# Last feed-forward of a four-layer kernel: its products moved to the first slots of the memory stage

## Chip, cores and metric

The kernel runs on one core of one Trainium2 chip. The metric is the device time of one execution, in microseconds. Each kernel was timed in several runs; the time before is 1814.58 us, the median of three runs (1812.86 to 1815.31).

## What is computed

Four residual sublayers follow each other; each is `x = x + layernorm(f(layernorm(x)))`. x has 4 batches of 512 rows and 256 columns, float32. The sublayers are a state-space mixer, a feed-forward with a Hadamard transform, an attention against a fixed memory, and a block of attention and eight experts. The change lies between the second and the third:

```
# second: feed-forward, hidden size 1024
hidden = silu(x @ W1.T) * (x @ W3.T)      # gate and up product
out = fwht(hidden) @ W2.T                 # transform of the 1024 columns
# third: memory attention, 8 heads of 128, memory of 256 rows, three steps
Q = layernorm(hidden) @ Wq.T ; K = mn @ Wk.T ; V = mn @ Wv.T
for _ in range(3):
    scores = einsum(xi, K) * beta
    w = entmax15(scores)                  # square(clip(x - tau, 0)), threshold tau by row
    xi = einsum(w, V)
out = xi @ Wo.T
```

## The kernel before

The rows lie in SBUF as `X`, 16 tiles of 128 rows (four tiles a batch, P = 128). The stages follow each other as blocks, each with an instruction queue written out for every engine: `layer0_block` (mixer and the feed-forwards of the first batches), `join_block` (memory weights folded into G1, G2, G3, and the gate products of the last batch), `memory_block`, `experts_block`. All waits are semaphores; nothing is scheduled by a planner.

`memory_block` works on 48 units. A unit is one step (of three) of one tile; four tiles go side by side in lanes, so unit m has lane m mod 4, and units 0 to 3 are first steps, 8 to 11 last steps, 12 to 15 first steps of the next four tiles. For a unit, TensorE makes the scores of 8 heads in four banks of PSUM (`score`, in pairs of heads), VectorE takes the eight largest of each row (`largest`, MAX8), GpSimd makes running sums of these, VectorE cuts at zero (`clear`), ScalarE takes a root, and VectorE takes the bound on the threshold (`bound`). From it GpSimd makes the first shift, and four passes refine it: ScalarE clips the scores with the shift (`clip`), VectorE takes mean and spread (`take_moments`), GpSimd makes a Newton step (`second_moment`, `newton`), with a root on ScalarE. The weights of the last pass are made by VectorE and GpSimd (`weights`), transposed by TensorE into banks TB and TB + 1 (4 and 5), and squared and copied to `wT` by ScalarE (`columns`). The next step of the tile takes its scores from `wT`; after the last step `output` makes the output rows into bank OUT (7), and `out_stats`, `out_norm` normalise and add them. Bank 6, ROWS, holds transposed input rows.

The order is by slots. Every engine runs a loop over n from -4 to 55, and each step of a unit has a fixed place in a slot with a fixed offset: in slot n TensorE makes the scores of unit n + 2 and the transposes of unit n - 1. VectorE in its slot n takes the largest of units n - 4 (last heads) and n - 3, the bound of unit n - 4, and so on; its slot n stands against TensorE's slot n - 6. An instruction waits for all that stand ahead of it in its engine's queue.

The last batch's feed-forward is spread over these slots. Its gates and its transposed rows are ready from `join_block`. `F_UP_AT` names the slots of the eight up products (0 to 7), `F_ROWS_AT` those of the four row products (8, 9, 14, 15):

- `f_up` (L1733): two matmuls of 512 columns into OUT, behind the scores of the slot.
- `f_hide` (L1353): VectorE multiplies the product into the gated rows.
- `f_rows` (L1747): eight matmuls of 256 columns into OUT for one tile, after all eight hides; the transform is in the weights by then.
- `f_stats_out` (L66, L68), `f_out_rstd` on GpSimd (L1555, L1557), `f_out` (L1365, L1368): normalise and add to X.
- The sync engine waits for `f_x_ready` of all four tiles and then loads the weights of the last stage.

`transpose` (L1723) puts one matmul on the identity ahead of each pair, the warm-up (L1716), except in some slots:

```
for _ in range(0 if a.m and Unit(a.m - 1).last or a.m + 1 in F_UP_AT + F_ROWS_AT else WARM[p]):
    pe.matmul(bank[:, TB + p % 2, 0:NMEM], ident[:], G1[:, 0, 0, :], start=True, stop=True)
```

A matmul in float32 appears as two records in the trace, each with its own weight load.

Of the kernel before, what the change touches and what calls it, by code (L numbers as in the profile page):

```python
# [18 lines left out]
ALU = mybir.AluOpType  # L19
# [3 lines left out]
P = 128  # L23
# [11 lines left out]
HT = HID // P  # L35
# [1089 lines left out]
DVE_HEADS = (0, 1, 2, 3, 4)  # L1125
POOL_HEADS = (5, 6, 7)
DVE_CLIPS = ((), (), (), (3,))
F_UP_AT = tuple(range(HT))
F_ROWS_AT = (8, 9, 14, 15)
FIRST_SLOT, LAST_SLOT = -4, TILES * STEPS - 1 + 8  # L1130

NPAIR = NHM // 2
# [19 lines left out]
def memory_block(nc, T, dram):  # L1152
# [7 lines left out]
    with ExitStack() as ctx:  # L1160
# [3 lines left out]
        def sem(name):  # L1164
# [3 lines left out]
        SC, TB, ROWS, OUT = 0, 4, 6, 7  # L1168
# [52 lines left out]
        f_up_done, f_hidden_ready, f_o_done, f_omv_ready, f_ors_ready, f_x_ready = (sem("f_" + n) for n in (  # L1221
            "up_done", "hidden_ready", "o_done", "omv_ready", "ors_ready", "x_ready"))
        block = ctx.enter_context(nc.Block())

        def out_rows(a):

# [30 lines left out]
        def _(dve):  # L1257
# [26 lines left out]
            def clear(a):  # L1284
                if not a.live:
                    return
                dve.wait_ge(room_ready, of_unit(a))
                dve.tensor_scalar(room[:, a.lane], room[:, a.lane], 0.0, None, ALU.max).then_inc(clear_ready, 1)

            def bound(a):  # L1290
                if not a.live:
                    return
                dve.wait_ge(back_ready, of_unit(a))
                dve.tensor_tensor(back[:, a.lane], back[:, a.lane], fold[0][:, a.lane, 0:NHM, PAD:], ALU.min)
                dve.drain()
                dve.tensor_reduce(neg8[:, a.lane], back[:, a.lane], AX.X, ALU.max, negate=True).then_inc(bound_ready, 1)
# [30 lines left out]
            def weights(a, *heads):  # L1327
                if not a.live:
                    return
                dve.wait_ge(shift_ready[PASSES - 1], of_unit(a))  # L1330
                for h in heads:
                    dve.tensor_scalar(u[a.lane][:, h, :], u[a.lane][:, h, :], shift[:, a.lane, h:h + 1], 0.0, ALU.add,  # L1332
                                      ALU.max).then_inc(dve_weights, 1)
# [12 lines left out]
                dve.drain()  # L1346
                dve.tensor_tensor(X[:, a.tile, :], X[:, a.tile, :], onorm[:], ALU.add).then_inc(x_ready, 1)

            def f_hide(s):
                if s in F_UP_AT:  # L1350
                    j = F_UP_AT.index(s)
                    dve.wait_ge(f_up_done, j + 1)
                    dve.tensor_tensor(hidden[j], bank[:, OUT, :], hidden[j], ALU.mult).then_inc(f_hidden_ready, 1)  # L1353

            def f_stats_out(s):
                if s in F_ROWS_AT:
                    t = F_ROWS_AT.index(s)
                    dve.wait_ge(f_o_done, t + 1)
                    norm_stats(dve, bank[:, OUT, 0:D], f_ostats, f_omv[:, t, :]).then_inc(f_omv_ready, 1)
# [26 lines left out]
            for n in range(FIRST_SLOT, LAST_SLOT + 1):  # L1386
                if n == LAST_SLOT - 3:
                    first_batch_stats()
                if n == LAST_SLOT - 1:
                    first_batch_rows()  # L1390
                largest(Unit(n - 4), 6, 7)
                take_moments(Unit(n - 5), 1, 0)
                invert(Unit(n - 6), 2)
                take_moments(Unit(n - 5), 1, 1, 2)
                weights(Unit(n - 7), 1, 2)
                tile_rows(Unit(n - 2))
                take_moments(Unit(n - 5), 1, 3)
                invert(Unit(n - 5), 1)
                weights(Unit(n - 7), 3)
                take_moments(Unit(n - 6), 3, 0)  # L1400
                f_hide(n - 6)
                f_stats_out(n - 6)
                tile_stats(Unit(n + 4))
                clear(Unit(n - 4))
                weights(Unit(n - 7), 4)
                if n - 7 == UNITS - 1:
                    weights(Unit(n - 7), 5, 6, 7)
                clip(Unit(n - 6), 3, 6)
                take_moments(Unit(n - 6), 3, 1)
                bound(Unit(n - 4))  # L1410
                clip(Unit(n - 6), 3, 7)
                take_moments(Unit(n - 6), 3, 2, 3)
                out_stats(Unit(n - 8))
                take_moments(Unit(n - 4), 0, 0)
                invert(Unit(n - 6), 3)
                take_moments(Unit(n - 4), 0, 1)
                take_moments(Unit(n - 5), 2, 0)
                out_norm(Unit(n - 8))
                f_out(n - 6)
                take_moments(Unit(n - 4), 0, 2)  # L1420
                largest(Unit(n - 3), 0, 1)
                take_moments(Unit(n - 4), 0, 3)
                weights(Unit(n - 6), 0)
                largest(Unit(n - 3), 2, 3)
                take_moments(Unit(n - 5), 2, 1)
                invert(Unit(n - 4), 0)
                take_moments(Unit(n - 5), 2, 2)
                largest(Unit(n - 3), 4)
                take_moments(Unit(n - 5), 2, 3)
                largest(Unit(n - 3), 5)  # L1430

        @block.gpsimd
        def _(pool):
# [77 lines left out]
            def start(a):  # L1511
                if not a.live:
                    return
                pool.wait_ge(bound_ready, of_unit(a))
                pool.tensor_tensor(shift[:, a.lane], neg8[:, a.lane], top[:, a.lane, :, 0], ALU.subtract).then_inc(start_ready, 1)  # L1515
# [62 lines left out]
            for n in range(FIRST_SLOT, LAST_SLOT + 1):  # L1578
                if n == LAST_SLOT - 3:
                    first_batch_norms()  # L1580
                add_room(Unit(n - 3))
                second_moment(Unit(n - 4), 1)
                step_back(Unit(n - 3))
                newton(Unit(n - 4), 1)
                start(Unit(n - 3))
                second_moment(Unit(n - 5), 3)
                tile_rstd(Unit(n + 3))
                out_rstd(Unit(n - 7))
                f_out_rstd(n - 5)
                newton(Unit(n - 5), 3)  # L1590
                if n - 5 != UNITS - 1:
                    weights(Unit(n - 5), 5)
                second_moment(Unit(n - 3), 0)
                if n - 5 != UNITS - 1:
                    weights(Unit(n - 5), 6)
                newton(Unit(n - 3), 0)
                if n - 5 != UNITS - 1:
                    weights(Unit(n - 5), 7)
                second_moment(Unit(n - 4), 2)
                centre(Unit(n - 2))  # L1600
                square(Unit(n - 2))
                running_sum(Unit(n - 2), 0)
                running_sum(Unit(n - 2), 1)
                newton(Unit(n - 4), 2)
                running_sum(Unit(n - 2), 2)
                mean_and_gap(Unit(n - 2))
                mean_square(Unit(n - 2))
                add_gap(Unit(n - 2))
# [73 lines left out]
        def _(pe):  # L1682
# [26 lines left out]
            def transpose(a, *pairs):  # L1709
                if not a.live:  # L1710
                    return
                for p in pairs:
                    if a.m * NPAIR + p >= 2:
                        pe.wait_ge(wT_ready, of_unit(a, NPAIR, p - 1))
                    for _ in range(0 if a.m and Unit(a.m - 1).last or a.m + 1 in F_UP_AT + F_ROWS_AT else WARM[p]):
                        pe.matmul(bank[:, TB + p % 2, 0:NMEM], ident[:], G1[:, 0, 0, :], start=True, stop=True)  # L1716
                    if any(h // 2 == p for h in dve_heads(a)):
                        pe.wait_ge(dve_weights, of_unit(a, len(DVE_HEADS), sum(h <= 2 * p + 1 for h in dve_heads(a))))
                    if any(h // 2 == p for h in pool_heads(a)):
                        pe.wait_ge(pool_weights, of_unit(a, len(POOL_HEADS), sum(h <= 2 * p + 1 for h in pool_heads(a))))  # L1720
                    for i in range(4):
                        h, piece = 2 * p + i // KN, i % KN
                        last = pe.transpose(bank[:, TB + p % 2, i * P:(i + 1) * P], u[a.lane][:, h, piece * P:(piece + 1) * P],  # L1723
                                            ident[:])
                    last.then_inc(wT_in_psum, 1)

            def f_up(s):
                if s in F_UP_AT:
                    j = F_UP_AT.index(s)
                    if j:  # L1730
                        pe.wait_ge(f_hidden_ready, j)
                    for k in range(KD):
                        last = pe.matmul(bank[:, OUT, :], w3[:, k, j * P:(j + 1) * P], f_xnT[:, k, :], start=k == 0,  # L1733
                                         stop=k == KD - 1)
                    last.then_inc(f_up_done, 1)

# [1126 lines left out]
```

## Time and profile before

| what | before |
|---|---|
| median of 3 runs | 1814.58 us |
| profiled execution | 1812.72 us |
| its span | 1810.9 us |
| mean granted clock of TensorE | 0.931 |
| TensorE busy, share of the span | 1557.9 us, 86% |
| VectorE busy | 1362.2 us, 75% |
| ScalarE busy | 1151.7 us, 64% |
| GpSimd busy | 751.9 us, 42% |

PE is TensorE's matmul queue, PEld its weight loads, DVE VectorE, ACT ScalarE, POOL GpSimd. PEclk is the granted clock as a share of full speed; it has two levels, 0.5 (1.2 GHz) and 1.0 (2.4 GHz), and values between are means over a stretch. Durations of neighbours on one engine overlap by a few hundredths, so what an instruction costs its queue is read from start to start. "idle before" is the engine's idle time ahead of an instruction, and the name behind the arrow is what ended it.

### The profile page before, as it was taken

How to read it: one execution, taken by the hardware profiler on the slowest of the kernel's cores; microseconds unless marked ns; L12 is line 12 of the kernel's file. 1: busy time of each engine (PE TensorE's matmuls, PEld its weight loads, DVE VectorE, ACT ScalarE, POOL GpSimd, SP SyncE). 2: the span in 40 equal slices, each digit the busy share in tenths (PEclk: the TensorE clock that was granted, in tenths of full speed). 3: DMA queues.
4: the chain of work that ended last, by engine and by line, in shares of the span. 5: the costliest groups of instructions: out<-in, count | busy, mean ns of one | idle time of the engine just before them, and what ended most of it. 6: DMA issues, size and time to landing. Idle time of an engine off the chain costs nothing. (4 is left out here: it accounts for less than half of the span.)

```text
span 1810.9 us, 25659 instructions
## 1 busy us (share of the span) xinstructions
PE 1557.9 (86%) x7346; PEld 1091.4 (60%) x7346; DVE 1362.2 (75%) x3568; ACT 1151.7 (64%) x2769; POOL 751.9 (42%) x2049
## 2 busy tenths in 40 slices
PE   5889999998577879877997789877779999999987
PEld 2546657466455668766786678666645556555554
DVE  6666757572489899999999999999644566767646
ACT  3243342413278888889989998999447565665630
POOL 3414224150356666677767776677310101001000
PEclk9699999998877899989998999899899999999989
DMA  5000000000000000030000000000000000000000
GB/s 231 1 1 1 1 1 1 1 1 0 1 1 1 1 1 1 1 112 1 1 1 1 1 1 1 1 1 1 1 1 1 1 1 1 1 13 1 13 1 24
DMA packets 6716, 19.21 MB, mean 11 GB/s; under 512 B 1072, under 2 KB 4144, under 8 KB 5296
## 3 DMA queue, kind: packets, MB, share of 16 engines
q1 hardware_dynamic: 6576, 17.58, 2.6%
q8 instruction: 60, 0.98, 0.2%
q14 instruction: 80, 0.66, 0.1%
HBM read 15.48 MB, written 2.10 MB: 10 GB/s over the span
## 5 line engine op out<-in xcount | busy, mean ns | idle before, releaser
L1316 DVE BATCH_NORM_STATS2 r_moments<-mem_arena 128x6 f32<-128x512 f32 x576 | 382.7, 683 | 4.2 <-ACT mem_arena L1638 4.1
L1638 ACT ACTIVATE mem_arena<-mem_arena,r_shift 128x256 f32<-128x256 f32 x792 | 351.3, 512 | 38.7 <-POOL r_shift L1533 38.7
L1706 PE MATMUL r_bank<-arena,r_wT 128*128 128x256 f32 x1024 | 243.8, 399 | 10.1 <-ACT mem_arena L1638 8.1
L1706 PEld LDWEIGHTS r_bank<-arena,r_wT 128*128 128x128 f32 x1024 | 203.1, 201 | 46.4 <-issue 17.2
L1723 PE MATMUL r_bank<-ident,mem_arena 128*128 128x128 f32 x576 | 107.1, 322 | 93.1 <-DVE mem_arena L1332 80.7
L1280 DVE MAX8 r_top<-r_bank 128x8 f32<-128x256 f32 x384 | 145.4, 417 | 26.5 <-PE r_bank L1706 24.3
L1723 PEld LDWEIGHTS r_bank<-ident,mem_arena 128*128 128x128 f32 x576 | 79.2, 165 | 131.0 <-DVE mem_arena L1332 65.7
L2293 ACT ACTIVATE arena<-arena,e_NM 128x512 f32<-128x512 f32 (+3 forms) x256 | 134.3, 558 | 29.2 <-DVE e_NM L1981 29.2
L1706 PE MATMUL r_bank<-arena,r_xnT 128*128 128x256 f32 x512 | 122.6, 401 | 18.2 <-ACT mem_arena L1638 17.0
L1981 DVE CUSTOM_DVE_ANT_0 arena<-e_banks,ffn_then_moe 128x512 f32<-128x512 f32 (+3 forms) x256 | 110.1, 485 | 28.9 <-PE e_banks L2498 28.5
L1316 DVE BATCH_NORM_STATS2 r_moments<-r_u 128x6 f32<-128x512 f32 x192 | 129.2, 684 | 2.5 <-ACT r_u L1638 2.4
L2304 ACT ACTIVATE mem_arena<-e_banks 128x512 f32<-128x512 f32 x160 | 92.4, 591 | 54.4 <-PE e_banks L2517 54.0
L1638 ACT ACTIVATE r_u<-r_u,r_shift 128x256 f32<-128x256 f32 x264 | 116.8, 512 | 13.4 <-POOL r_shift L1533 13.4
L1540 POOL TENSOR_SCALAR mem_arena<-mem_arena,r_shift 128x256 f32<-128x256 f32 x108 | 123.4, 1143 | 3.8 <-issue 0.2
L1706 PEld LDWEIGHTS r_bank<-arena,r_xnT 128*128 128x128 f32 x512 | 102.2, 202 | 35.9 <-issue 20.8
L1767 PE MATMUL r_bank<-arena,r_wT 128*128 128x256 f32 x512 | 120.1, 384 | 0.0
L1638 ACT ACTIVATE mem_arena<-r_bank,r_shift 128x256 f32<-128x256 f32 x288 | 116.3, 486 | 1.3 <-POOL r_shift L1515 1.3
L1656 ACT ACTIVATE r_wT<-r_bank 128x512 f32<-128x512 f32 x192 | 109.5, 610 | 10.7 <-PE r_bank L1723 10.7
L2517 PEld LDWEIGHTS e_banks<-ident,arena 128*128 128x128 f32 x640 | 74.1, 140 | 49.7 <-issue 24.8
L2200 POOL TENSOR_TENSOR ffn_then_moe<-e_ms,eps 128x4 f32<-128x4 f32 x4 | 0.8, 199 | 247.8 <-ACT e_act_gate L2263 247.8
L1767 PEld LDWEIGHTS r_bank<-arena,r_wT 128*128 128x128 f32 x512 | 96.1, 193 | 11.9
L2517 PE MATMUL e_banks<-ident,arena 128*128 128x128 f32 x640 | 91.4, 274 | 6.8 <-ACT arena L2293 4.6
(324 smaller groups left out, 3315.9 us busy)
## 6 DMA issues: line engine op xcount, KB each, us to landing
ffn_then_moe<-in_w SPq DMA_DIRECT2D x3, 1024.0 KB, 14.4
out_x<-X SPq DMA_DIRECT2D x4, 512.0 KB, 2.9
X<-in_x SPq DMA_DIRECT2D x1, 1536.0 KB, 11.4
w_in<-in_w_in SPq DMA_DIRECT2D x1, 1156.0 KB, 6.2
mem_arena<-in_wq SPq DMA_DIRECT2D x1, 1024.0 KB, 16.6
mem_arena<-in_wo SPq DMA_DIRECT2D x1, 1024.0 KB, 20.9
ffn_then_moe<-in_gate SPq DMA_DIRECT2D x1, 1024.0 KB, 7.3
ffn_then_moe<-in_up SPq DMA_DIRECT2D x1, 1024.0 KB, 9.3
```

What stands on the lines that cost most here:

```text
L1280: last = dve.max(top[:, a.lane, h, :], scores[:, h, :])
L1316: last = dve.bn_stats(moments[:, a.lane, 2 * p:2 * p + 2, :].rearrange("p two c -> p (two c)"), u[a.lane][:, 2 * p:2 * p + 2, :].rearrange ...
L1540: pool.tensor_scalar(u[a.lane][:, h, :], u[a.lane][:, h, :], shift[:, a.lane, h:h + 1], 0.0, ALU.add, ALU.max).then_inc(pool_weights, 1)
L1638: last = act.activation(u[a.lane][:, h, :], u[a.lane][:, h, :] if k else scores[:, h, :], ACT.Relu, bias=shift[:, a.lane, h:h + 1])
L1656: act.activation(wT[:, a.lane, 2 * p:2 * p + 2, :, :], bank[:, TB + p % 2, :], ACT.Square).then_inc(wT_ready, 1)
L1706: last = pe.matmul(scores[:, h, :], lhs, (G1 if a.first else G2)[:, h, i, :], start=i == 0, stop=i == 1)
L1723: last = pe.transpose(bank[:, TB + p % 2, i * P:(i + 1) * P], u[a.lane][:, h, piece * P:(piece + 1) * P], ident[:])
L1767: last = pe.matmul(out_rows(a), wT[:, a.lane, h, piece, :], G3[:, h, piece, :], start=h == 0 and piece == 0, stop=h == NHM - 1 and piece = ...
L1981: last = dve.tensor_tensor_reduce(out=seen[:, j, c0:c0 + width], in0=bank[LOOK + j][:, c0:c0 + width], in1=T["mask_q"][:, S - width:], sca ...
L2293: last = act.activation(rows_p[:, j, P_AT[i]:P_AT[i] + width], seen[:, j, c0:c0 + width], ACT.Exp, scale=-1.0, bias=NM[:, i, j:j + 1])
L2304: act.activation(PT[kb][:, :, (i - kb) * P:(i - kb + 1) * P], bank[t_bank(a, g, r)].rearrange("p (j q) -> p j q", j=4), ACT.Copy).then_inc ...
L2517: last = pe.transpose(o[:, j * P:(j + 1) * P], rows_p[:, j, P_AT[i] + kb * P:P_AT[i] + (kb + 1) * P], ident[:])
```

## The change

`F_UP_AT` becomes the slots -2, -2, -2, -1, -1, -1, 0, 0: three, three and two up products behind the scores of units 0, 1 and 2. They go to three banks in turn, OUT, TB and TB + 1, which are free before the first transposes, and product j waits for the hide of product j - 3 only. The row products move to slots 2, 4, 6 and 8. In VectorE's slot the hides get three places (behind `clear`, behind `bound`, behind the third first-pass moments); the row statistics move from ahead of `clear` to behind `out_norm`, and the row outputs come one slot later. GpSimd's root for the rows moves one slot later and up to just behind `start`. The first transposes wait for all eight hides. By the condition of the warm-up, slots 1, 3, 5, 7, 9, 14 and 15 now have it; slots 2, 4, 6 and 8 still have none.

```
-F_UP_AT = tuple(range(HT))
-F_ROWS_AT = (8, 9, 14, 15)
+F_UP_AT = (-2, -2, -2, -1, -1, -1, 0, 0)
+F_ROWS_AT = (2, 4, 6, 8)
+        def ups_in(s):
+            return [j for j in range(HT) if F_UP_AT[j] == s]
+        def up_bank(j):
+            return (OUT, TB, TB + 1)[j % 3]
 # VectorE
-            def f_hide(s):
-                if s in F_UP_AT:
-                    j = F_UP_AT.index(s)
+            def f_hide(s, i):
+                for j in ups_in(s)[i:i + 1]:
                     dve.wait_ge(f_up_done, j + 1)
-                    dve.tensor_tensor(hidden[j], bank[:, OUT, :], ...
+                    dve.tensor_tensor(hidden[j], bank[:, up_bank(j), :], ...
...
-                f_hide(n - 6)
-                f_stats_out(n - 6)
                 tile_stats(Unit(n + 4))
                 clear(Unit(n - 4))
+                f_hide(n - 6, 0)
                 weights(Unit(n - 7), 4)
...
                 bound(Unit(n - 4))
+                f_hide(n - 6, 1)
                 clip(Unit(n - 6), 3, 7)
...
                 out_norm(Unit(n - 8))
-                f_out(n - 6)
                 take_moments(Unit(n - 4), 0, 2)
+                f_hide(n - 6, 2)
+                f_stats_out(n - 6)
+                f_out(n - 7)
                 largest(Unit(n - 3), 0, 1)
 # GpSimd
                 start(Unit(n - 3))
+                f_out_rstd(n - 6)
                 second_moment(Unit(n - 5), 3)
                 tile_rstd(Unit(n + 3))
                 out_rstd(Unit(n - 7))
-                f_out_rstd(n - 5)
 # TensorE
             def transpose(a, *pairs):
...
+                if a.m == 0 and 0 in pairs:
+                    pe.wait_ge(f_hidden_ready, HT)
             def f_up(s):
-                if s in F_UP_AT:
-                    j = F_UP_AT.index(s)
-                    if j:
-                        pe.wait_ge(f_hidden_ready, j)
+                for j in ups_in(s):
+                    if j >= 3:
+                        pe.wait_ge(f_hidden_ready, j - 2)
                     for k in range(KD):
-                        last = pe.matmul(bank[:, OUT, :], w3[...], f_xnT[:, k, :], ...
+                        last = pe.matmul(bank[:, up_bank(j), :], w3[...], f_xnT[:, k, :], ...
```

## Rows read from the trace of the kernel before

**Rows 1.** The page's 40 equal slices of the span, busy tenths, VectorE's line.
```profile
DVE  6666757572489899999999999999644566767646
```

**Rows 2.** Windows from one `bound` to another: length, each engine's busy time, PEclk.
```profile
480.85:497.89 17.04, 9.84 (x34) 7.82 (x34) 9.67 (x22) 7.69 (x21) 5.59 (x21) 0.80 0.00 0
497.89:515.46 17.57, 11.02 (x36) 8.28 (x36) 13.41 (x31) 13.46 (x36) 6.56 (x27) 0.79 0.00 0
515.46:533.21 17.75, 13.05 (x48) 9.69 (x48) 16.02 (x39) 13.88 (x37) 11.31 (x36) 0.79 0.01 2
533.21:638.91 105.70, 83.52 (x313) 61.38 (x312) 97.35 (x242) 89.25 (x234) 69.45 (x220) 0.81 0.00 1
638.91:690.67 51.76, 44.01 (x208) 36.38 (x208) 49.74 (x125) 45.51 (x121) 35.66 (x112) 0.95 0.00 1
742.53:796.25 53.72, 43.44 (x190) 34.65 (x188) 51.52 (x132) 44.63 (x117) 35.43 (x112) 0.89 0.20 66
843.44:859.11 15.67, 12.62 (x56) 10.18 (x57) 15.52 (x40) 14.74 (x39) 12.04 (x39) 0.89 0.00 1
1102.65:1119.85 17.20, 16.14 (x83) 13.89 (x82) 16.54 (x43) 15.26 (x42) 11.88 (x37) 1.00 0.01 1
```

**Rows 3.** VectorE's groups in 480.85-533.21, 533.21-656.66 and 827.77-890.54: MAX8, its idle time last.
```profile
L1280 DVE MAX8 r_top<-r_bank 128x8 f32<-128x256 f32 x24 | 9.3, 422 | 8.2 <-PE r_bank L1706 7.9
L1280 DVE MAX8 r_top<-r_bank 128x8 f32<-128x256 f32 x56 | 21.9, 422 | 8.8 <-PE r_bank L1706 7.5
L1280 DVE MAX8 r_top<-r_bank 128x8 f32<-128x256 f32 x32 | 11.9, 413 | 0.0
```

**Rows 4.** VectorE's timeline: start, duration, instruction, idle time before it in brackets.
```profile
565.90 0.67 DVE L1353 TENSOR_TENSOR ffn_then_moe<-r_bank,ffn_then_moe 128x512 f32<-128x512 f32 x1
566.49 0.41 DVE L1261 BATCH_NORM_STATS2 r_stats<-X 128x6 f32<-128x256 f32 x1
...
757.68 0.41 DVE L66 BATCH_NORM_STATS2 ffn_then_moe<-r_bank 128x6 f32<-128x256 f32 x1
...
758.26 0.40 DVE L1261 BATCH_NORM_STATS2 r_stats<-X 128x6 f32<-128x256 f32 x1
...
763.81 0.54 DVE L1365 TENSOR_SCALAR ffn_then_moe<-r_bank,ffn_then_moe 128x256 f32<-128x256 f32 x1
...
764.93 0.69 DVE L1316 BATCH_NORM_STATS2 r_moments<-mem_arena 128x6 f32<-128x512 f32 x1
...
841.92 0.20 DVE L1288 TENSOR_SCALAR r_room<-r_room 128x64 f32<-128x64 f32 x1 [0.44 <-POOL r_room L1503]
```

**Rows 5.** TensorE's timeline: whole score products (L1706), an up product (L1733), a row product (L1747).
```profile
465.37 9.30 PE L1706 MATMUL r_bank<-arena,r_xnT 128*128 128x256 f32 x32
...
482.37 9.40 PE L1706 MATMUL r_bank<-arena,r_xnT 128*128 128x256 f32 x32 [6.09 <-ACT mem_arena L1638]
...
614.15 1.88 PE L1733 MATMUL r_bank<-ffn_then_moe 128*128 128x512 f32 x4
...
649.17 3.62 PE L1747 MATMUL r_bank<-ffn_then_moe 128*128 128x256 f32 x16
...
658.22 7.15 PE L1706 MATMUL r_bank<-arena,r_wT 128*128 128x256 f32 x32 [0.92 <-ACT mem_arena L1638]
...
761.88 9.59 PE L1706 MATMUL r_bank<-arena,r_wT 128*128 128x256 f32 x32 [0.46 <-ACT mem_arena L1638]
...
976.96 7.14 PE L1706 MATMUL r_bank<-arena,r_wT 128*128 128x256 f32 x32 [0.40 <-ACT mem_arena L1638]
```

**Rows 6.** Timeline around the first `bound`, and GpSimd's at a row's root.
```profile
480.54 0.23 DVE L1294 TENSOR_TENSOR r_back<-r_back,r_fold 128x64 f32<-128x64 f32 x1 [0.72 <-POOL r_back L1509]
...
482.26 2.16 DVE L1316 BATCH_NORM_STATS2 r_moments<-mem_arena 128x6 f32<-128x512 f32 x3 [1.19 <-ACT mem_arena L1638]
...
658.43 0.20 POOL L1521 TENSOR_TENSOR r_spread<-r_moments,r_inv_n 128x8 f32<-128x8 f32 x1 [1.23 <-DVE r_moments L1316]
...
659.09 0.19 POOL L1555 TENSOR_TENSOR ffn_then_moe<-ffn_then_moe,eps 128x1 f32<-128x1 f32 x1
```

More of the change, by code:

```diff
@@ L1347, in out_norm @@
                 dve.tensor_tensor(X[:, a.tile, :], X[:, a.tile, :], onorm[:], ALU.add).then_inc(x_ready, 1)
-            def f_hide(s):
-                if s in F_UP_AT:
-                    j = F_UP_AT.index(s)
+            def f_hide(s, i):
+                for j in ups_in(s)[i:i + 1]:
                     dve.wait_ge(f_up_done, j + 1)
-                    dve.tensor_tensor(hidden[j], bank[:, OUT, :], hidden[j], ALU.mult).then_inc(f_hidden_ready, 1)
+                    dve.tensor_tensor(hidden[j], bank[:, up_bank(j), :], hidden[j], ALU.mult).then_inc(f_hidden_ready, 1)
             def f_stats_out(s):
@@ L1727, in f_up @@
             def f_up(s):
-                if s in F_UP_AT:
-                    j = F_UP_AT.index(s)
-                    if j:
-                        pe.wait_ge(f_hidden_ready, j)
+                for j in ups_in(s):
+                    if j >= 3:
+                        pe.wait_ge(f_hidden_ready, j - 2)
                     for k in range(KD):
-                        last = pe.matmul(bank[:, OUT, :], w3[:, k, j * P:(j + 1) * P], f_xnT[:, k, :], start=k == 0,
+                        last = pe.matmul(bank[:, up_bank(j), :], w3[:, k, j * P:(j + 1) * P], f_xnT[:, k, :], start=k == 0,
                                          stop=k == KD - 1)
```

## The prediction, made before the result was known

> **What bounds the kernel now.** I read the page's slices first: VectorE stands at nine tenths only between about slice 12 and slice 27, the memory stage, where the change lies [rows 1]. Then one table of windows, cut at the instruction that opens the loop of one unit, `bound` (its reduction writes r_neg). I call the time from `bound` of unit m to `bound` of unit m+1 period m. A period of the plain pattern takes 15.67 us with 15.52 of VectorE; a period with an output product takes 17.20; the periods in which the feed-forward runs take 17.04 to 17.75 each, six of them (3 to 8) 105.70, that is 17.62 each, and they show a granted clock of 0.79 to 0.81 where the plain one shows 0.89 and the output one 1.00 [rows 2]. So two things make these periods long: VectorE's extra instructions, and something that goes with the clock.
>
> The second is seen in the groups of VectorE by line: before MAX8, the first reader of the scores, it sits idle 8.2 us in periods 0 to 2 and 8.8 in periods 3 to 9, but 0.0 in four plain periods [rows 3]. The releaser is the score product. Its 32 records take 7.14 us in a plain period and 9.59, 9.40 or 9.30 where the periods around show the lower mean clock [rows 2, 5]. The loop that sets a period is then: bound, shift on GpSimd, clips on ScalarE, scores on TensorE, MAX8 on VectorE, a row of small operations on GpSimd, clear, bound. VectorE's queue runs through all of it. Only between MAX8 of the last heads and `clear` is there slack: a plain period shows 0.44 us idle before clear [rows 4].
>
> **The price list.** On VectorE, from start to start of the next instruction [rows 4]: hide product 566.49 - 565.90 = 0.59 us; row statistics 758.26 - 757.68 = 0.58; row output, two instructions, 764.93 - 763.81 = 1.12. On TensorE: one up product, 4 records, 1.88; one row product, 16 records, 3.62 [rows 5].
>
> **Where the change puts them.** Before, products 0 to 7 are hidden in periods 1 to 8, ahead of `clear`, where the 0.44 of slack can take most of one; in periods 3 to 6 the next tiles' statistics (0.58 by their place behind the hide) use that slack up. Rows are done in periods 9 and 10 and again in 15 to 17. After, hides 0 to 2 fall in the end of the fill and period 0, hides 3 to 5 in periods 0 and 1, hides 6 and 7 in periods 1 and 2. Row products run in periods 3, 5, 7, 9, their statistics in 4, 6, 8, 10 and their outputs in 5, 7, 9, 11. The warm-up products on the identity come back ahead of the transposes of slots 1, 3, 5, 7, 9, 14 and 15; slots 2, 4, 6 and 8 go without.
>
> **Periods 0 to 2 (now 52.36 us).** TensorE is idle from the end of the first scores, 465.37 + 9.30 = 474.7, to the next ones at 482.37 [rows 5]: three up products (5.64) fit in these 7.7 us and leave 2.1 to 2.5 of idle. Hide 0 sits between clear and bound of unit 0, where VectorE waits 0.72 for GpSimd anyway; hide 1 sits behind bound, before a wait of 1.19 for the clips [rows 6]; hide 3 finds a like gap one unit later. These three cost nothing; were the gaps gone they would cost 0.59 each. Hide 2 stands before a MAX8 that waits for scores. What TensorE gains: with at most 2.5 us of idle before them, do the second scores run at the full clock? The nearest row is the score product at 658.22, which began 5.4 us after a row product ended at 652.8, with transposes in between, and took 7.15 [rows 5]; the other bound is 9.40 as now. So between 0 and 2.25; I take 1.4, nearer to the row, since the clock can still fall in the middle. Period 1: hide 6 comes behind clear in a period that is nearly full, 0.5 more than now; hide 5 goes into the MAX8 stall; of the stall I take 0.8 away. Net 0.3 (-0.5 to 1.5). Period 2: hide 7 adds 0.59 less about 0.1 of the old one, inside a stall; the gap ahead of the scores is some 5.6 us, so half the chance of a full clock. Net 0.35 (-0.5 to 1.0). Sum: 2.05 gained (-1.0 to 4.75).
>
> **Periods 3 to 8 (now 105.70).** Six plain periods 94.02; tile statistics beyond the slack 4 x (0.58 - 0.44) = 0.56; row statistics in three periods, now behind bound where nothing hides them, 1.74; row outputs in two 2.24. Stalls: after a slot with warm-up products none (plain rows), after a row slot without them half the scores come cold as I read it: two score products in [rows 5] follow a row product, and one took 7.15, the other (761.88) 9.59. The statistics stand ahead of MAX8 and swallow 0.58 of a stall. I put 0.4 on each of three periods and 0.3 on period 3. Sum 100.1, gain 5.6. Bounds: all cold 3.4, none 7.1.
>
> **Periods 9 to 11 (now 51.76).** 47.01 plain, one statistics 0.58, two outputs 2.24, residue 0.4: 50.2, gain 1.5 (0.5 to 1.9).
>
> **Periods 12 to 14** are not touched: 0.
>
> **Periods 15 to 17 (now 53.72).** The last two tiles' rows leave: 17.20 + 2 x 15.67 + 2 x 0.14 = 48.8, gain 4.8 (3.5 to 5).
>
> **Edits at nothing.** The row's root on GpSimd (two instructions on one column; the first takes 0.19, and the pair with its drain I estimate at 0.9, under five times that) goes ahead of second_moment, where GpSimd waits 1.23 for VectorE [rows 6]; without that wait it would hold ScalarE's root and the clips by up to 0.9 in four periods, 3.6. What it waits for, the statistics, is then a period old. TensorE's new wait for all eight hides in slot 1 stands before transposes that wait for later weights; queued behind it are only these. The bank waits j - 2 are met when the product three before is hidden, before the next scores. SyncE's wait for four finished rows is met in period 11 instead of 17, so the expert weights (the 66 GB/s of [rows 2]) load earlier, long before anyone asks for them; SyncE has nothing else queued there.
>
> **Sum.** 2.05 + 5.6 + 1.5 + 0 + 4.8 = 14.0 us. The profiled execution took 1812.72 us with a span of 1810.9; it would become 1798.7 with 1796.9. It lies 1.9 below the median of the three runs, so the median goes from 1814.58 to 1800.6. Bounds of the parts together: 6.4 to 18.8 gained.
>
> **A rule weighed.** The score products of one shape take 7.14 us or 9.59, and the periods differ with the granted clock [rows 2, 5]. The Trainium skill (TensorE: Matmul & The Clock Gate, Part 1, "What's actually happening") says of such ramps "don't fit to a specific cold count", because the same kernel shows different counts from run to run, and puts them under 1% of a kernel's span. By it the clock would be left out of the sum and only VectorE's instructions counted; the third rival below is worked out for that. The trace disagrees in so far as the stall before MAX8 adds up to 17.0 us over ten periods here and to 0.0 over four plain ones [rows 3].
>
> **Rivals.** A measurement of this kernel can tell about 0.2%, 3.6 us.
> 1. The clock stays low behind the row slots and in the fill: all lower bounds, gain 6.4, 1808.2. For it: the row product's neighbour at 761.88 took 9.59. Against: 658.22. Chance 0.20.
> 2. It stays full throughout: gain 18.8, 1795.8. For it: idle of TensorE shrinks everywhere. Against: plain periods too show 0.89. Chance 0.09.
> 3. The clock gives nothing, and the stalls only move to other periods. Then only the hides count: now four at 0.59 and four at 0.14 (2.9), afterwards two at about 0.55 (1.1), rows unchanged: gain 1.8, 1812.8, no change that can be measured. Against it: [rows 3]. Chance 0.06.
> 4. Slower: the up products hold up the fill. Its scores are a chain of latencies, and if a group of products ends after the next clips are ready, every product is exposed: 8 x 1.88 on TensorE and 8 x 0.59 on VectorE, 19.8, against 11.9 gained later, hence 1822. It decides from the point where 5.64 exceeds the gap of 7.7. It does not by 2 us, and the third group is of two only. Chance 0.04.
> The forecast, 1797.5 to 1805 as its own range, has 0.61. The range of 8 in 10 goes from 1796 to 1808.5. Faster by over 0.2%: 0.61 + 0.20 + 0.09 = 0.90; same 0.06; slower 0.04.
>
> **What would show it.** Periods 3 to 8 sum to about 100 with a clock near 0.9; MAX8's idle in periods 3 to 9 falls from 8.8 to under 3; periods 16 and 17 are plain; the six hides from 0 to 5 lie before 502 us. The second scores, near 482, take under 9 us. If period 0 stays at 17 the fill gives nothing; if odd periods stall before MAX8, the warm-up products are not what keeps the clock; if GpSimd's second_moment starts later than 1.5 us after r_shift, the moved root costs. Wrong altogether if the gain lies below 6 or if a new wait for ScalarE appears in VectorE's take_moments.

## The result, and the profile after

The changed kernel takes 1803.15 us, the median of four runs (1798.87 to 1806.71), against 1814.49 (1812.86 to 1815.31): ratio 0.9938, interval 0.9926 to 0.9950, 11.3 us faster. Forecast were 1800.6 and 14.0 us. The profiled execution is one of the slower of its four: 1804.84 us with a span of 1803.1, 7.8 less than that of before. (One run of all below, of the kernel without any warm-up, took 2350.6 us at a mean granted clock of 0.631, against 0.905 to 0.909 in its other three, and is left out of that kernel's figures.)

First the windows of the changed kernel, cut at `bound` as in [rows 2]: periods 0, 1, 2, then 3 to 8, 9 to 11 and 15 to 17.

```profile
482.54:499.02 16.48, 14.20 (x46) 9.75 (x46) 11.46 (x26) 7.69 (x21) 5.61 (x21) 0.90 0.00 0
499.02:515.33 16.31, 10.58 (x40) 7.52 (x40) 14.34 (x32) 13.56 (x37) 6.76 (x28) 1.00 0.00 0
515.33:533.78 18.45, 14.37 (x50) 11.64 (x50) 15.97 (x39) 13.82 (x37) 11.04 (x35) 0.72 0.01 2
533.78:637.00 103.22, 83.82 (x360) 66.72 (x360) 96.48 (x247) 89.12 (x234) 71.16 (x224) 0.88 0.00 1
637.00:687.87 50.87, 43.96 (x201) 35.46 (x202) 49.15 (x123) 45.57 (x121) 35.83 (x112) 0.93 0.20 60
739.45:788.48 49.03, 38.80 (x174) 31.91 (x172) 48.19 (x125) 44.38 (x117) 34.25 (x108) 0.87 0.00 1
```

| periods | before | after | gained | forecast |
|---|---|---|---|---|
| 0 to 2 | 52.36 | 51.24 | 1.1 | 2.05 |
| 3 to 8 | 105.70 | 103.22 | 2.5 | 5.6 |
| 9 to 11 | 51.76 | 50.87 | 0.9 | 1.5 |
| 12 to 14 | 51.86 | 51.58 | 0.3 | 0 |
| 15 to 17 | 53.72 | 49.03 | 4.7 | 4.8 |
| sum | 315.40 | 305.94 | 9.5 | 14.0 |

What brings these 9.5 us to the 7.8 of the span lies outside: `bound` of unit 0 comes 1.7 us later (482.54 against 480.85), as the stage's first row statistics already do (461.66 against 459.95), behind code that is the same; periods 18 to 46 give 0.5, and what follows takes 0.4 more.

Inside, the periods alternate. These are the windows of periods 3, 4 and 5:

```profile
533.78:549.49 15.71, 13.43 (x66) 11.17 (x66) 15.53 (x40) 14.76 (x39) 11.20 (x36) 1.00 0.00 0
549.49:567.98 18.49, 14.99 (x54) 11.99 (x54) 16.30 (x42) 14.88 (x39) 11.23 (x36) 0.72 0.01 1
567.98:584.65 16.67, 13.62 (x66) 11.10 (x66) 16.41 (x42) 14.87 (x39) 11.93 (x38) 0.99 0.00 1
```

Period 5, with a row output, takes 16.67 us; period 4, with the row statistics, which cost half as much, takes 18.49, with the clock at 0.72. TensorE's timeline in the same stretch, as in [rows 5] (L1714 is the score product, L1756 the row product, L1733 the transposes, L1726 a warm-up):

```profile
535.34 7.14 PE L1714 MATMUL r_bank<-arena,r_wT 128*128 128x256 f32 x32 [0.40 <-ACT r_u L1646]
542.33 3.62 PE L1756 MATMUL r_bank<-ffn_then_moe 128*128 128x256 f32 x16
545.78 0.60 PE L1733 MATMUL r_bank<-ident,mem_arena 128*128 128x128 f32 x4
547.02 0.63 PE L1733 MATMUL r_bank<-ident,mem_arena 128*128 128x128 f32 x4 [0.64 <-DVE mem_arena L1339]
548.52 0.63 PE L1733 MATMUL r_bank<-ident,mem_arena 128*128 128x128 f32 x4 [0.88 <-issue]
549.52 0.66 PE L1733 MATMUL r_bank<-ident,mem_arena 128*128 128x128 f32 x4 [0.37 <-ACT r_wT L1664]
551.05 10.02 PE L1714 MATMUL r_bank<-arena,r_wT 128*128 128x256 f32 x32 [0.87 <-ACT mem_arena L1646]
560.91 0.59 PE L1726 MATMUL r_bank<-arena,ident 128*128 128x256 f32 x2
564.05 1.12 PE L1733 MATMUL r_bank<-ident,mem_arena 128*128 128x128 f32 x4 [2.55 <-DVE mem_arena L1339]
564.96 1.06 PE L1726 MATMUL r_bank<-arena,ident 128*128 128x256 f32 x2
565.82 1.06 PE L1733 MATMUL r_bank<-ident,mem_arena 128*128 128x128 f32 x4
566.67 0.82 PE L1726 MATMUL r_bank<-arena,ident 128*128 128x256 f32 x2
567.33 0.60 PE L1733 MATMUL r_bank<-ident,mem_arena 128*128 128x128 f32 x4
568.02 0.70 PE L1726 MATMUL r_bank<-arena,ident 128*128 128x256 f32 x2
568.55 0.60 PE L1733 MATMUL r_bank<-ident,mem_arena 128*128 128x128 f32 x4
569.54 7.14 PE L1714 MATMUL r_bank<-arena,r_wT 128*128 128x256 f32 x32 [0.39 <-ACT mem_arena L1646]
```

Without warm-ups, sparse transposes (0.6 us each with gaps) lead into scores at 551.05 that take 10.02 us; the transposes with warm-ups stand close together from 564.05 and begin cold (1.12 us instead of 0.60), by 567.33 they are back at 0.60, and the next scores, at 569.54, take 7.14. Scores of periods 6, 8 and 10 took 9.51, 9.26 and 9.16; those of 5, 7 and 9, 7.14. Before MAX8, as in [rows 3], VectorE still idles in periods 3 to 9:

```profile
L1287 DVE MAX8 r_top<-r_bank 128x8 f32<-128x256 f32 x56 | 21.5, 422 | 4.6 <-PE r_bank L1714 4.4
```

### The profile page after: what moved, and what is told of

Read it like the earlier page. It is cut to its first block and busy times, and to the rows that moved or that the text cites. A ratio compares the mean times of both kernels' runs of the same rounds, so it can differ in the third digit from the quotient of the medians.

```text
span 1803.1 us, 25750 instructions
## 1 busy us (share of the span) xinstructions
PE 1563.6 (87%) x7402; PEld 1098.8 (61%) x7402; DVE 1362.3 (76%) x3568; ACT 1151.3 (64%) x2769; POOL 753.7 (42%) x2049
## 5 line engine op out<-in xcount | busy, mean ns | idle before, releaser
L1714 PE MATMUL r_bank<-arena,r_wT 128*128 128x256 f32 x1024 | 237.7, 392 | 9.0 <-ACT mem_arena L1646 6.8
L1714 PEld LDWEIGHTS r_bank<-arena,r_wT 128*128 128x128 f32 x1024 | 198.7, 197 | 42.4 <-issue 14.9
L1733 PE MATMUL r_bank<-ident,mem_arena 128*128 128x128 f32 x576 | 105.9, 318 | 89.4 <-DVE mem_arena L1339 86.8
L1733 PEld LDWEIGHTS r_bank<-ident,mem_arena 128*128 128x128 f32 x576 | 80.1, 164 | 125.8 <-DVE mem_arena L1339 89.1
L1714 PE MATMUL r_bank<-arena,r_xnT 128*128 128x256 f32 x512 | 120.9, 397 | 11.6 <-ACT mem_arena L1646 10.7
L1776 PE MATMUL r_bank<-arena,r_wT 128*128 128x256 f32 x512 | 119.9, 383 | 0.0
L1714 PEld LDWEIGHTS r_bank<-arena,r_xnT 128*128 128x128 f32 x512 | 101.0, 200 | 29.0 <-issue 14.4
L1776 PEld LDWEIGHTS r_bank<-arena,r_wT 128*128 128x128 f32 x512 | 96.0, 193 | 11.8
```

Source lines behind the costliest of these rows:

```text
L1714: last = pe.matmul(scores[:, h, :], lhs, (G1 if a.first else G2)[:, h, i, :], start=i == 0, stop=i == 1)
L1776: last = pe.matmul(out_rows(a), wT[:, a.lane, h, piece, :], G3[:, h, piece, :], start=h == 0 and piece == 0, stop=h == NHM - 1 and piece = ...
```

## The experiments

Period sums below come from each run's own profile, with the same cuts. The ratios are to the kernel before on the same chip. Its medians there were 1814.29 us for the first four experiments, 1815.19 for the next four and 1816.28 for the last two.

**The clock in the row slots.** The warm-ups go into slots 2, 4, 6 and 8 as well:

```
-  0 if a.m and Unit(a.m - 1).last or a.m + 1 in F_UP_AT + F_ROWS_AT else WARM[p]
+  0 if a.m and Unit(a.m - 1).last else WARM[p]
```

> The changed kernel with the warm-up matmuls also in slots 2, 4, 6 and 8, the ones with a row product. Theory (the even periods stall because their scores start at the low clock): the scores of periods 4, 6, 8 and 10 fall from 9 to 10 us to about 7.2, the 5.3 us of idle before MAX8 in these four periods goes, and the kernel is 4 to 5.5 us faster than the changed one, about 1798. Rival (the row product of 3.62 us itself is too much for TensorE's queue, the transposes come late): the warm-ups add 8 records a slot to the same queue, the stalls stay or grow, and the time is 0 to 3 us longer, 1803 to 1806.

1797.64 us, ratio 0.9908 (0.9895 to 0.9922). Here are its windows for periods 3 to 8 and 9 to 11, and MAX8 in periods 3 to 9:

```profile
532.66:630.44 97.78, 82.68 (x385) 66.52 (x384) 95.59 (x246) 89.09 (x234) 70.96 (x224) 0.95 0.00 1
630.44:680.03 49.59, 43.18 (x211) 34.89 (x210) 48.92 (x123) 45.31 (x121) 35.82 (x112) 1.00 0.21 65
```

```profile
L1287 DVE MAX8 r_top<-r_bank 128x8 f32<-128x256 f32 x56 | 21.0, 417 | 0.0
```

TensorE has more records (385 against 360) and the stretch is 5.4 us shorter; the stalls are gone and the even periods take 16.26, 16.29, 16.23, 16.24, with scores of 7.14 to 7.15 us. The rival, TensorE's queue too long, falls.

**No warm-up that came back.** The condition ends in `a.m + 1 in (1, 2, 3, 4, 5, 6, 7, 8, 9, 14, 15)`.

> The changed kernel without any of the warm-ups that came back: slots 1 to 9, 14 and 15 go without, as before the change. Theory (half of the gain was the clock's): the odd periods 3, 5, 7, 9 and periods 15 to 17 get cold scores too, each with 0.5 to 1.5 us of stall, so the time is 3 to 6 us above the changed kernel, 1806 to 1809. Rival (the gain is that of fewer VectorE instructions in full periods): no difference, 1803, as the stall only moves.

1808.42 us, ratio 0.9964 (0.9952 to 0.9977). Periods 3 to 8 take 103.06, 9 to 11 50.88, 15 to 17 51.36, 308.68 in all. Moving the products without warm-ups gives about 6 us. The time is where the theory put it, and the odd periods are longer as it said (17.42, 17.17, 17.04, 17.06, with scores of 8.59 to 8.94 us where the changed kernel has 7.14), but the even ones are shorter than in the changed kernel (17.23 instead of 18.49, with scores of 8.76 instead of 10.02), which it did not foresee. The waits before MAX8 in periods 3 to 9 that the view puts down to the scores sum to only 2.3 us; with the many short ones, under 0.15 us each, its idle time is 3.9.

**The kernel before, with warm-ups.** The edit of the first experiment, made in the kernel before.

> The kernel before, up and row products where they were, but with the warm-ups in slots 1 to 9, 14 and 15. Theory (clock): of the 8.8 us of idle before MAX8 in periods 3 to 9 and the 0.9 in period 16 most goes, 6 to 8 us faster than before, about 1807. Rival (the stalls there are TensorE's load by the products): no gain, 1814, or slower.

1800.59 us, ratio 0.9923 (0.9910 to 0.9935): twice the gain that was expected. Its windows for periods 3 to 8 and 9 to 11, and MAX8 in 3 to 9:

```profile
533.39:630.22 96.83, 80.29 (x360) 58.56 (x360) 95.81 (x242) 88.54 (x234) 69.37 (x220) 1.00 0.00 1
630.22:680.40 50.18, 45.85 (x225) 37.85 (x226) 49.53 (x125) 45.44 (x121) 35.60 (x112) 1.00 0.00 1
```

```profile
L1280 DVE MAX8 r_top<-r_bank 128x8 f32<-128x256 f32 x56 | 21.0, 416 | 0.0
```

No product was moved, and the clock goes from 0.81 to 1.00 and six periods from 105.70 to 96.83. With warm-ups everywhere, the move of the products then adds what lies between 1800.59 and 1797.64, 3 us (the intervals overlap). By the two profiles it comes from the fill (periods 0 to 2, 52.35 here and 51.29 there) and from the rows that left periods 15 to 17 (52.02 and 48.97); periods 3 to 8, which the up products left, gain nothing, since the rows took their place (96.83 and 97.78).

**The up products alone.** Rows as before, in slots 8, 9, 14 and 15; up products, banks and hides as changed; warm-ups return in slots 1 to 7.

```
-F_ROWS_AT = (2, 4, 6, 8)
+F_ROWS_AT = (8, 9, 14, 15)      # f_stats_out, f_out(n - 6), f_out_rstd(n - 5) where they were
```

> The up products as in the changed kernel (three banks, slots -2 to 0), the row products, their statistics, roots and outputs as before (slots 8, 9, 14, 15); warm-ups in slots 1 to 7. Theory: periods 3 to 8 become plain ones with tile statistics, 94.6 us for the six against 105.7 before and 103.2 in the changed kernel, while periods 9, 10 and 15 to 17 stay as before (35.0 and 53.7). That is 11 to 12 us faster than before, about 1803, level with the changed kernel: moving the rows is worth nothing by itself. Rival (moving the rows is what pays): 1808 or more.

1800.66 us, ratio 0.9920 (0.9906 to 0.9933), 2 us less than expected. Periods 3 to 8 take 94.25 us, 15.71 each, nothing but plain ones; 9 to 11 50.13, 15 to 17 53.54. The move of the rows is worth nothing here: against the changed kernel's own profile it costs 9.7 us in periods 3 to 11 (6.3 against its second profile, below) and saves 4.5 in 15 to 17. Rows and up products apart, with warm-ups in all slots, were not run.

**The gap at the end of the fill.** To the first experiment's kernel, at slot 1 of TensorE:

```
+  if n == 1:
+      pe.wait_ge(f_hidden_ready, 6)
+      keep_warm(11, TB + 1)          # matmuls on the identity
   score(Unit(n + 2), 0, 1, 2, 3)
```

> The kernel with warm-ups in the row slots too, plus 11 matmuls on the identity ahead of the scores of slot 1, into the bank that hide 5 has freed. In the changed kernel and in that one TensorE idles 5.5 us there and the scores of period 2 take 10.05 us, with 1.8 to 1.9 us of idle before MAX8. Theory (clock): 11 matmuls of 0.43 us fill the gap, these scores take 7.1 us, period 2 goes from 18.5 to about 16.4, and the time falls by 1.5 to 2 us to about 1796. Rival (period 2 is long by its two hides and a latency chain): period 2 stays above 18, the time at 1797.6 or above.

1794.75 us, ratio 0.9889 (0.9873 to 0.9906). Period 2, which took 18.49 in the first experiment:

```profile
515.88:532.13 16.25, 11.27 (x54) 8.51 (x52) 15.71 (x40) 13.82 (x37) 11.00 (x35) 1.00 0.00 1
```

Its scores take 7.14 us instead of 10.09, as the theory has it. The period shows the gain; the medians, from two chips, do not by themselves, since the intervals of the ratios overlap.

**The start of the stage.** `keep_warm(8, TB)` ahead of TensorE's first slot.

> The same, plus 8 matmuls on the identity as the first instructions of TensorE in the memory stage. Theory: the first scores start at the low clock and take 9.3 us, all of it a latency that the whole pipeline waits for; with TensorE kept busy from 460 us they take about 7.2, and everything behind comes 2 us earlier, about 1794. Rival: the eight run at the low clock (0.85 us each, 6.8 in all) and hold up the first transposes of rows, which start at 463.7; then 0 to 3 us are lost instead, 1796 to 1799.

This kernel has the matmuls of the one before it too. 1794.37 us, ratio 0.9884 (0.9870 to 0.9899). TensorE's first instructions of the stage; L1783 is `keep_warm`, L1698 transposes rows:

```profile
462.57 3.69 PE L1783 MATMUL r_bank<-arena,ident 128*128 128x256 f32 x16 [1.82 <-PEq L2737]
466.10 0.38 PE L1698 MATMUL r_bank<-ident,r_xn 128*128 128x128 f32 x2
467.47 0.41 PE L1698 MATMUL r_bank<-ident,r_xn 128*128 128x128 f32 x2 [0.99 <-ACT r_xnT L1628]
467.72 7.07 PE L1714 MATMUL r_bank<-arena,r_xnT 128*128 128x256 f32 x32
```

The first scores take 7.07 instead of 9.55, and from the stage's first instruction to the first `bound` it is 18.40 us instead of 21.01. But period 1 now takes 17.70 instead of 16.33 and period 3 16.14 instead of 15.71: the clock falls at other places. The scores of period 1 take 8.83 us (granted 0.81) instead of 7.14, and the transposes ahead of those of period 3 take 1.03 to 1.11 us each instead of 0.60 to 0.66, so that these scores start 2.1 us behind `bound` instead of 1.6. Why it falls there no run separates. In the time 0.4 us is left, less than can be told. The 1794 of the theory came out by luck, because the kernel without these eight matmuls already took 1794.75; the 2 us that they were to give did not come, and neither did the loss of the rival.

**Statistics back ahead of `clear`.** In the last kernel `f_stats_out(n - 6)` stands before `tile_stats`.

> The same with the row statistics moved back ahead of clear, into the slot's slack (the row outputs still one slot later). Price list: they now cost 0.58 us in each of periods 4, 6, 8, 10; there they would cost 0.58 in periods 3 and 5, which have tile statistics, and 0.14 in 7 and 9: 0.9 us gained. Rival (statistics right behind the row product wait for it): periods 3, 5, 7, 9 grow by a wait of VectorE for TensorE (L66 with an idle time), 0 to 2 us lost.

1793.07 us, ratio 0.9875 (0.9861 to 0.9890), the lowest median of all. Periods 4, 6, 8 and 10 come to 15.69, 15.73, 15.67 and 15.67, but 3, 5 and 9 grow to 16.62, 17.22 and 17.40. Periods 0 to 17 sum to 298.28 against 298.53: the direction is the expected one, the size (0.3 for 0.9) not, and the medians' 1.3 us are within their spread. The clock is not in it: the scores of periods 3 to 10 all take 7.14 us. Period 5 grows by 0.58, the price of the statistics; periods 3 and 9 hold besides an idle time of VectorE of 0.43 and 0.42 us each, ended by nothing that the profile shows (the second one before L68, in the statistics themselves). That of period 3:

```profile
546.33 0.22 DVE L1303 TENSOR_REDUCE r_neg<-r_back 128x8 f32<-128x64 f32 x1 [0.43 <-issue]
```

**No warm-up anywhere.** In the kernel before, `WARM = (0, 0, 0, 0)`.

> The kernel before without any warm-up at all. It prices them where the change does not reach: 22 periods outside the feed-forward have them. Theory: a cold score product costs a period 0.3 to 1.5 us through MAX8, as in periods 3 to 9 before; so 8 to 25 us more than before, 1822 to 1840, with a granted clock near 0.8 in the plain periods. Rival (the plain periods are long on other grounds and have slack): within 4 us of 1814.

1840.19 us, the median of three runs (1839.94 to 1845.15), against 1815.19: ratio 1.0138, 25 us slower, the upper end of the range; the spans of the two profiles differ by 27.2. Periods 18 to 46 take 495.03 us against 467.83; most of the plain ones take 17.01 to 17.16 instead of 15.65 to 15.70. A window of 17 us in it shows the clock of the feed-forward slots of before:

```profile
863.00:880.00 17.00, 13.00 (x55) 10.10 (x56) 16.80 (x44) 16.36 (x46) 12.29 (x40) 0.80 0.00 0
```

**The changed kernel again**, for the spread of its runs.

> The changed kernel once more, unaltered. Its four runs spread over 7.8 us and its profiled execution entered the memory stage 1.7 us later than that of before (461.66 against 459.95), in code that is the same. If that start is chance, it will come out on the other side as often, the periods 0 to 17 will again sum to about 306 us, and the median will lie at 1803, give or take 2. If the change itself moves the start, it is again near 461.7.

1801.95 us (1799.0 to 1804.45), ratio 0.9920 (0.9907 to 0.9932). The stage's first instruction starts at 460.42, between the two earlier ones, so that start is chance. But its periods 3 to 8 are not those of the first profile:

```profile
532.70:632.84 100.14, 79.57 (x361) 63.02 (x360) 96.20 (x246) 89.12 (x234) 71.01 (x224) 0.93 0.00 1
```

```profile
547.43 0.63 PE L1733 MATMUL r_bank<-ident,mem_arena 128*128 128x128 f32 x4 [0.87 <-issue]
548.43 0.66 PE L1733 MATMUL r_bank<-ident,mem_arena 128*128 128x128 f32 x4 [0.37 <-ACT r_wT L1664]
549.96 7.14 PE L1714 MATMUL r_bank<-arena,r_wT 128*128 128x256 f32 x32 [0.87 <-ACT mem_arena L1646]
```

The same instructions at the same distance (0.87 us of idle) lead here to scores of 7.14 us, where the first profile has 10.02: period 4 takes 16.26 against 18.49, and periods 6, 8 and 10 take 17.46, 17.42 and 17.27. The sum of periods 0 to 17 is 302.58, not the 306 expected.

**Warm-ups ahead of the last two transposes only.** `WARM = (0, 0, 1, 1)` in the first experiment's kernel.

> The kernel with warm-ups in all slots, but only ahead of the last two of the four transposes. Theory A (what counts is that TensorE is busy just before the scores): little is lost, the scores of the even periods stay at 7.1 to 7.5 us, the time within 2 us of 1797.6. Theory B (the clock needs the whole chain of transposes and warm-ups): a good part of the scores comes at the low clock, plain periods grow towards the 17.1 that they have with no warm-ups, and the time goes to 1805 or more.

1799.55 us, ratio 0.9908 (0.9893 to 0.9923), the ratio of the full set. Periods 3 to 8 take 97.94 (97.78 with four), but period 1 takes 17.72 instead of 16.33, now and then a plain period takes 16.1 to 16.7, and periods 18 to 46 sum to 471.15 us against 467.31 with four. So the equal ratio flatters it. From the first `bound` to the end of period 46 its profile takes 771.2 us, 4.7 more than with four warm-ups and 12.0 less than before; what follows, which no edit reached, happened to take 2.8 less (544.4 against 547.2). Half the warm-ups, close to the scores, keep most of the gain, about 12 of 17 us, not all.

## Why the prediction was right, and where it was not

The direction, the size within its range and the two causes hold. 11.3 us came for 14.0 in the first set of runs, 14.3 in the second (1816.28 less 1801.95). In the first profile the difference has a name, the stalls of the even periods; in the second, with smaller stalls, periods 3 to 8 gain 5.6 us and all of 0 to 17 12.8. That the second set lies on the forecast is luck: it is the same kernel, and the stalls were not priced as something that varies.

- **What bounds the stage.** The loop through bound, clips, scores and MAX8 with VectorE's queue in it holds: most plain periods stayed at 15.65 to 15.70 in every kernel with all four warm-ups and went to about 17.1 without any, and in periods 3 to 9 the idle time before MAX8 is 8.8 us before, 4.6 in the changed kernel, 1.8 in its second profile, 3.9 with no new warm-up and 0.0 with warm-ups everywhere. It does not follow the sum of the periods in step: with no new warm-up it is less than in the changed kernel while periods 3 to 8 are as long (103.06 and 103.22).
- **The stall behind a row slot, the term that was off.** I gave it 0.4 us in each of periods 4, 6 and 8 and in 9 to 11, "half the scores come cold". Taken the same way (period less plain, statistics and 0.14), the first profile has 2.1, 1.6, 1.5 and 1.4, 6.6 us instead of 1.6; the gain of periods 3 to 8, 2.5, lies even under the 3.4 that I gave for "all cold". In the second profile period 4 stalls not at all and 6, 8 and 10 by about 1. Warm-ups in the same slots take it to zero. So the term has no single value, and the two rows I went by could not give it: they stand in other slots, and there they repeat (7.14 and 9.47 with the up products alone, 7.14 and 9.44 with no warm-up anywhere). Whether the clock also explains how far the times of one kernel spread stays open: the changed kernel's runs spread over 7.8 and 5.5 us and those of the first experiment over 2.7, but those with the gap filled over 7.2.
- **Period 2.** The "half the chance of a full clock" came out cold: 18.45, 0.7 lost for 0.35 gained. Period 1 made up for it, 16.31 for the 17.3 forecast: 2.5 us of idle did leave the scores at 7.14. Two more profiles with this fill have the same pair (16.33 and 18.49, 16.31 and 18.51); three others, from the kernels with no new warm-up, the up products alone and the last two transposes, have 17.69 to 17.72 and 17.64 to 17.73. Period 0 gave 0.6 for 1.4, its scores took 8.83: the clock fell in their middle (granted 0.81 over them), as feared.
- **The hides at nothing.** VectorE's timeline at `bound` of unit 0:

```profile
481.43 0.68 DVE L1359 TENSOR_TENSOR ffn_then_moe<-r_bank,ffn_then_moe 128x512 f32<-128x512 f32 x1
482.24 0.23 DVE L1301 TENSOR_TENSOR r_back<-r_back,r_fold 128x64 f32<-128x64 f32 x1
482.54 0.22 DVE L1303 TENSOR_REDUCE r_neg<-r_back 128x8 f32<-128x64 f32 x1
482.68 0.68 DVE L1359 TENSOR_TENSOR ffn_then_moe<-r_bank,ffn_then_moe 128x512 f32<-128x512 f32 x1
483.95 2.17 DVE L1323 BATCH_NORM_STATS2 r_moments<-mem_arena 128x6 f32<-128x512 f32 x3 [0.59 <-ACT mem_arena L1646]
```

Against [rows 6], the wait of 0.72 is gone, that of 1.19 is 0.59, and `bound` and the moments keep their distance.

- **Prices.** Statistics 0.58 in the even periods: 16.26 less 15.70 is 0.56. Row outputs came cheaper: 16.67 less 15.70 is 0.97, and start to start they take 573.02 - 572.08 = 0.94, since the addition took 0.43 here and 0.59 at 764.42 us in the kernel before. The hides cost what I said: with warm-ups in the kernel before, periods 3 to 6 take 16.30 to 16.31, 0.6 over a plain one. The tile statistics did not: I took 0.14 beyond the slack in each of four periods, and with the up products alone these take 15.68 to 15.70, like plain ones. For periods 15 to 17 my own terms add up to 48.82, a gain of 4.9, not 4.8; 4.7 came.
- **GpSimd's root moved up costs nothing**: in period 5 second_moment still waits 0.37 us for VectorE behind it, and starts 1.47 us after r_shift.

```profile
568.49 0.18 POOL L1563 TENSOR_TENSOR ffn_then_moe<-ffn_then_moe,eps 128x1 f32<-128x1 f32 x1
568.82 0.56 POOL L1565 TENSOR_TENSOR ffn_then_moe<-ffn_then_moe,half_neg 128x1 f32<-128x1 f32 x1
569.75 0.20 POOL L1529 TENSOR_TENSOR r_spread<-r_moments,r_inv_n 128x8 f32<-128x8 f32 x1 [0.37 <-DVE r_moments L1323]
```

- **The rule weighed.** The Trainium skill's advice not to fit a count of cold matmuls (TensorE: Matmul & The Clock Gate, Part 1) is borne out: the same scores took 10.02 and 7.14 us in two executions of one kernel. The Trainium skill's figure in the same place, under 1% of a kernel's span for the ramp, does not carry over to this loop: no warm-up anywhere costs 1.4% of the time here. Leaving the clock out of the sum would have given 1.8 us of gain for the 11.3 measured. The third rival falls, and so does the fourth, with the scores of unit 1 starting 2.5 us after the three products had ended.
- **The other signs.** MAX8's idle time in periods 3 to 9 was to fall under 3 us: 4.6 in the first profile, 1.8 in the second. Period 17 is plain (15.69), period 16 nearly (16.11). Hide 5 starts at 503.20, not before 502, in a stage that started 1.7 us late. VectorE's waits for ScalarE in take_moments, in periods 0 to 9, fell from 3.1 to 1.9 us.
- **What I did not see**: that the move was not needed for most of it. A condition that keeps warm-ups out of slots with products held 13.7 us in the kernel before. I priced the warm-ups as a side effect of the move, stall by stall, and never the condition by itself.

What stays open: why the clock falls where it does. That is all that separates the changed kernel's two profiles, and it makes the even periods of the second experiment shorter than those of the changed kernel (scores of 8.6 to 8.8 us instead of 9.3 to 10.0 in periods 4, 6 and 8). Open too are the two idle times of 0.4 us in the kernel with the early statistics, which are not the clock's.

## What to carry to other kernels

This loop of latencies through TensorE had two speeds, 15.7 and 17.1 us a period, and the filler matmuls that keep the faster one were worth more (13.7 us) than a better place for useful work (5.9 us without them, 3 with them). In such a loop, try them just before the product that everything waits for, also in slots that seem busy enough. When an edit changes a condition that other instructions hang on, price that part by itself, and first. A part whose clock came out either way in two rows is a term with two values, not with their mean: widen by it, or remove it. And equal medians of two kernels can hide a loss in the stage that was edited and a chance gain in one that was not: compare the stage as well.

## What the runs showed of the hardware

- 32 records of 256 columns took 7.07 to 7.15 us at a granted clock of 1.00 throughout, and 7.1 to 10.1 when it was at 0.5 for a part of them, the longer the lower its mean over them (0.99 down to 0.70).
- Eight more records of matmuls on the identity in a slot took no time from the rest: at full clock throughout its scores, period 4 took 16.26 us without them (the changed kernel again) and 16.26 with them (the first experiment).
- Two executions of the same instructions, with the same idle gaps ahead of the scores, differed by 2.2 us in one period (18.49 and 16.26).
- An earlier start did not simply shift the rest: eight matmuls gained 2.6 us ahead of the first `bound` and 1.8 were given back in periods 1 and 3, where the clock was now low in places where it had been full.
